# Layer 0's scan sum y stored by pairs of batches, and ScalarE's wait moved to the scatter's own semaphore

## The reference

```python
xn = layernorm(x)
delta = softplus(xn @ W_xproj[:64].T @ W_dt.T + b_dt)        # per token and channel
for t in range(512):                                           # along each batch
    h = exp(delta[t] * A) * h + (delta[t] * xn[t]) * B[t]      # N = 16 states a channel
    y[t] = sum_n h[n] * C[t, n]
x = x + y + xn * D_param + experts(xn)                         # 4 of 16 experts a token
```

## Time and profile before

| | |
|---|---|
| median of 3 runs | 1266.36 us (1265.95 to 1267.10) |
| the profiled execution, its own time | 1271.14 us |
| its span, first to last instruction | 1269.4 us |
| busy: PE, DVE, ACT, POOL | 1032.2, 916.2, 489.1, 466.8 us |
| DMA engines' time taken by the software queue | 33.5% of the span |
| adds into y, scatters and gathers of layer 0 | 32, 80, 80 |

### The profile page before, as it was taken

One profiled execution on the slowest core, in us unless ns is written; L12 is line 12 of the kernel. 1 busy time (PEld: TensorE's weight loads), 2 busy tenths in 40 slices (PEclk: granted clock), 3 DMA queues, 4 the chain that ended last, 5 costly groups with the idle time before them and its releaser, 6 DMA issues.

```text
span 1269.4 us, 18530 instructions
## 1 busy us (share of the span) xinstructions
PE 1032.2 (81%) x6024; PEld 600.7 (47%) x6024; DVE 916.2 (72%) x1506; ACT 489.1 (39%) x1114; POOL 466.8 (37%) x333
## 2 busy tenths in 40 slices
PE   3987997888887878773587778989889988888895
PEld 2354455444444444442434444555545555455453
DVE  4767768899888889897486655766768666755576
ACT  2200235455544445451130144544554444434442
POOL 0000103788888788762270003222313222123310
PEclk9988999898988889995888889989999999899897
DMA  7950443878878787899620134433433333234413
GB/s 228 366 128 0 126 79 105 148 129 148 147 139 159 127 155 134 147 148 213 134 63 1 26 79 97 97 81 81 100 89 81 90 81 79 64 81 106 95 28 133
DMA packets 111188, 143.25 MB, mean 113 GB/s; under 512 B 30023, under 2 KB 97335, under 8 KB 110903
## 3 DMA queue, kind: packets, MB, share of 16 engines
q0 software_dynamic: 34464, 77.92, 33.5%
q1 hardware_dynamic: 76630, 64.14, 18.1%
HBM read 72.80 MB, written 39.46 MB: 88 GB/s over the span
## 4 chain that ended last, share of the span: by engine, by line
PE 33%; DVE 11%; DMA 5%; ACT 4%; issue 3%; POOL 1%; SPq 1%; ACTq 0%; DVEq 0%; POOLq 0%
PE bank L1846 5%; PE bank L1434 4%; PE bank L1427 4%; PE bank L1890 3%; DMA sum<-yo,to_i 3%; DVE cv L2091 2%; PE bank L698 2%; PE bank L1829 2%; PE bank L1912 2%; PE bank L1876 2%; PE bank L1838 2%; PE bank L1870 1%; PE bank L686 1%; DMA x<-sum 1%; DVE areaD L2036 1%
## 5 line engine op out<-in xcount | busy, mean ns | idle before, releaser
L1500 POOL DMA_INDIRECT sum<-yo,to_i x48 | 76.9, 1602 | 361.4 <-ACT yo L1454 359.1
L1164 POOL DMA_INDIRECT sum<-yo,to_i x80 | 156.0, 1950 | 47.5 <-issue 39.9
L1171 POOL DMA_INDIRECT xg<-xn_d,token_i x80 | 103.1, 1289 | 174.7 <-DVE to_i L460 92.2
L1011 PE MATMUL bank<-areaA,xgT 128*128 x320 | 133.0, 545 | 15.2 <-issue 8.8
L1028 PE MATMUL bank<-areaA,hidT 88*128 x320 | 96.7, 427 | 41.5 <-ACT hidT L1076 29.8
L2036 DVE TENSOR_TENSOR areaD<-areaD,gb 128x512 f32<-128x512 f32 x128 | 87.5, 689 | 41.9 <-ACT areaD L1983 32.8
L1144 DVE TENSOR_TENSOR_SCAN xnT<-areaB,xnT 128x1024 f32<-128x1024 f32 x42 | 96.3, 2292 | 3.3
L1028 PEld LDWEIGHTS bank<-areaA,hidT 88*128 88x128 f32 x320 | 57.7, 201 | 76.5 <-issue 71.4
L1983 ACT ACTIVATE areaD<-bank 128x512 f32<-128x512 f32 x128 | 76.1, 594 | 44.7 <-PE bank L1838 42.6
L1011 PEld LDWEIGHTS bank<-areaA,xgT 128*128 128x128 f32 x320 | 62.9, 215 | 61.6 <-issue 46.6
L686 PE MATMUL bank<-xnT,areaB 128*128 128x512 f32 x192 | 86.8, 599 | 0.8 <-DVE y L716 0.8
(11 more groups left out here) (338 smaller groups left out, 2201.9 us busy)
## 6 DMA issues: line engine op xcount, KB each, us to landing
y<-xnT POOLq DMA_DIRECT2D x21, 1024.0 KB
wst<-gu_f SPq DMA_DIRECT2D x96, 176.0 KB
y<-areaB POOLq DMA_DIRECT2D x11, 1024.0 KB
wst<-down_f SPq DMA_DIRECT2D x48, 176.0 KB
areaA<-in_gu SPq DMA_DIRECT2D x2, 2816.0 KB
gu_f<-in_gu POOLq DMA_DIRECT2D x1, 5632.0 KB, 16.8
sum<-yo SPq DMA_DIRECT2D x2, 2176.0 KB, 16.2
down_f<-in_down POOLq DMA_DIRECT2D x1, 2816.0 KB, 22.5
```

Of the source, the lines that this page charges most:

```text
L1011: last = nc.tensor.matmul(bank[:, GB + q % 2, 0:2 * FI], xgT[:, q % 2, k, :], wgu0_of(e, k), start=(k == 0), stop=(k == KD - 1))
L1164: nc.gpsimd.indirect_dma_start(sum0_d[q % 2], bass.IndirectOffsetOnAxis(ap=to_i[:, q:q + 1], axis=0), yo[:, q % 5, :], None, compute_op=AL ...
L1171: nc.gpsimd.indirect_dma_start(xg[:, q % 5, :], None, xn_d[0], bass.IndirectOffsetOnAxis(ap=token_i[:, q:q + 1], axis=0)).then_inc(s.gathe ...
L1500: nc.gpsimd.indirect_dma_start(sum1_d, bass.IndirectOffsetOnAxis(ap=to_i[:, q:q + 1], axis=0), yo[:, q % 4, :], None, compute_op=ALU.add). ...
```

## The change

`y` becomes [128, 2 pairs of batches, 2 halves, 1024 tokens]. A pair's two halves are then adjacent in a partition, and both sides of the add's DMA are one run of 8192 bytes a partition: 128 runs instead of 256, the same bytes. What writes and reads `y` elsewhere (the first fill on ACT, the 32 transposing products of `scan_out_tensor` on PE) follows the new layout. `yo_free` is dropped: ACT waits for the landing of scatter q - 5 itself, on the DMA's semaphore, and POOL no longer counts `yo_free`, in both layers.

```diff
--- before.py
+++ after.py
@@ -159,7 +159,7 @@
             self.tanh_ready, self.hid_ready, self.hT_full = sem(f"tanh_ready{l}"), sem(f"hid_ready{l}"), sem(f"hT_full{l}")
             self.hT_ready, self.y_full, self.y_ready = sem(f"hT_ready{l}"), sem(f"y_full{l}"), sem(f"y_ready{l}")
             self.gathered = [sem(f"gathered{l}_{s}") for s in range(RING[l])]
-            self.combined, self.yo_free = sem(f"combined{l}"), sem(f"yo_free{l}")
+            self.combined = sem(f"combined{l}")
             self.added = [sem(f"added{l}_{k}") for k in range(2 - l)]
             self.sum_out = sem(f"sum_out{l}")
             if l == 1:
@@ -757,8 +757,8 @@
         parts = sb("parts", [3 * 2 * N0, T], BF16, c0)
         delta = sb("delta", [P, 2, T], F32, c0)
         dx = sb("dx", [P, 2, T], F32, c0)
-        y = sb("y", [P, 2, T], F32, c0)
-        shT0 = y[:, :, :].rearrange("p h t -> p (h t)").rearrange("p (f t) -> p f t", t=512)
+        y = sb("y", [P, 2, 2, LB], F32, c0)
+        shT0 = y[:, :, :, :].rearrange("p b h t -> p (b h t)").rearrange("p (f t) -> p f t", t=512)
         drT = dx[0:R0, 1, :]
         odd_sum = areaA[:, 0:TT * D].rearrange("p (t d) -> p t d", d=D)
         after = M0 + m0["words"]
@@ -1079,7 +1079,7 @@
 
             act.wait_ge(s.y_full, q + 1)
             if q > 4:
-                act.wait_ge(s.yo_free, q - 4)
+                act.wait_ge(s.added[(q - 5) % 2], 16 * ((q - 5) // 2 + 1))
             nc.scalar.activation(yo[:, q % 5, :], bank[:, HY, 0:D], ACT.Copy, scale=slot_w[:, q % 5:q % 5 + 1]).then_inc(s.y_ready, 1)
 
         def layer0_scalar(act):
@@ -1089,7 +1089,7 @@
             decay(act, 0)
             act.wait_ge(s.sh_out, NB * 4)
             for hf in range(2):
-                nc.scalar.activation(y[:, hf, :], xnT[:, hf, :], ACT.Copy, scale=d_par[:, hf:hf + 1]).then_inc(y_init, 1)
+                nc.scalar.activation(y[:, :, hf, :], xnT[:, hf, :].rearrange("p (b t) -> p b t", t=LB), ACT.Copy, scale=d_par[:, hf:hf + 1]).then_inc(y_init, 1)
                 if hf == 0:
                     xT_copy(act, 0)
             act.wait_ge(delta_ready, 4)
@@ -1149,18 +1149,17 @@
 
         def add_scan(pool, pair):
 
-            n, hf, at = unit_views(2 * pair)
             pool.wait_ge(hc_ready, 2 * pair + 2)
             if pair > 1:
                 pool.wait_ge(y_added[pair % 2], 16 * (pair // 2))
-            nc.gpsimd.dma_start(y[:, :, at], h_pair[pair % 3], accum_op=ALU.add).then_inc(y_added[pair % 2], 16)
+            nc.gpsimd.dma_start(y[:, pair % 2, :, :].rearrange("p h t -> p (h t)"), h_pair[pair % 3].rearrange("p h t -> p (h t)"),
+                                accum_op=ALU.add).then_inc(y_added[pair % 2], 16)
 
         def scatter_add(pool, q):
 
             pool.wait_ge(s.y_ready, q + 1)
             if q > 1:
                 pool.wait_ge(s.added[q % 2], 16 * (q // 2))
-                pool.sem_inc(s.yo_free, 1)
             nc.gpsimd.indirect_dma_start(sum0_d[q % 2], bass.IndirectOffsetOnAxis(ap=to_i[:, q:q + 1], axis=0),
                                          yo[:, q % 5, :], None, compute_op=ALU.add).then_inc(s.added[q % 2], 16)
 
@@ -1214,7 +1213,7 @@
                     pe.wait_ge(x_back[t // 4], 32)
                 nc.tensor.matmul(bank[:, XB + t % 4, 0:D], ident[:, :], odd_sum[:, t, :], start=True, stop=False)
                 for hf in range(2):
-                    last = nc.tensor.matmul(bank[:, XB + t % 4, hf * P:(hf + 1) * P], y[:, hf, t * P:(t + 1) * P], ident[:, :],
+                    last = nc.tensor.matmul(bank[:, XB + t % 4, hf * P:(hf + 1) * P], y[:, t // 8, hf, t % 8 * P:(t % 8 + 1) * P], ident[:, :],
                                             start=False, stop=(hf == 1))
                 last.then_inc(yT_full, 1)
 
@@ -1450,7 +1449,7 @@
             if part == 2 and 1 <= q <= NT1:
                 act.wait_ge(q1.y_full, q)
                 if q > 4:
-                    act.wait_ge(q1.yo_free, q - 4)
+                    act.wait_ge(q1.added[0], 16 * (q - 4))
                 nc.scalar.activation(yo[:, (q - 1) % 4, :], bank[:, EB + (q - 1) % 2, 0:D], ACT.Copy,
                                      scale=slot_w[:, (q - 1) % 4:(q - 1) % 4 + 1]).then_inc(q1.y_ready, 1)
             if part == 2 and q < NT1:
@@ -1496,7 +1495,6 @@
             pool.wait_ge(q1.y_ready, q + 1)
             if q:
                 pool.wait_ge(q1.added[0], 16 * q)
-                pool.sem_inc(q1.yo_free, 1)
             nc.gpsimd.indirect_dma_start(sum1_d, bass.IndirectOffsetOnAxis(ap=to_i[:, q:q + 1], axis=0),
                                          yo[:, q % 4, :], None, compute_op=ALU.add).then_inc(q1.added[0], 16)
```

## The result

The changed kernel takes 1248.3 us (median of four runs, 1245.6 to 1256.5) against 1266.2 for the kernel before beside it (1264.9 to 1267.1): a ratio of 0.9867, with a 95% interval of 0.9831 to 0.9903. It is 1.3% faster. I had forecast 1265.0 with a range that ended at 1261.8, so the sign was within what I allowed and the size was not.

What follows compares the result with a forecast made beforehand. The prediction took the loop as paced by DVE and its round trip through PE and ACT. Terms 0 + 0 + 0.9 + 0.5 = 1.4 us took 1266.36 to 1265.0 us, range 1261.8 to 1267.8.

Steps and rivals of the forecast that it cites:

- The semaphore, 0: Both layers: ACT's wait for yo_free was never held (17 ns each time), so dropping it gains 0.
- The add on the DMA engines, 5.8 to 5.57 us: Each add of y: 8 KB packets save 0.23 us, taken as 0.25, with bounds of 0 and 0.7.
- rival C: Add's transfer and POOL issue both save near their upper bounds: 3.5 to 4.4 us, 1262.8 to 1262.0; chance 0.31.
- Rival B: Packets get no cheaper, as the queue cuts 8 KB runs or the skill's rule holds: 0.1 us, 1266.2; chance 0.14.
- The rule of the Trainium skill: Small descriptors cost extra only in HBM, not within on-chip memory; by it the add keeps its 5.8 us.
- The forecast's straight line: DMA packet time from 1 and 4 KB: fixed part 0.029 us a packet, so 0.696 us for 8 KB.
- The issue on POOL, 0.2 us less: POOL's issue of each add, 1.28 to 1.9 us, falls by 0.2 with 128 fewer runs; bounds 0 and about 0.65.
- The loop's end, 1.4 us: Adds 27 to 29 and the loads behind them: PE's step 8 comes 0.9 + 0.5 = 1.4 us sooner.
- the engines' start: DMA engines at the loop's end: with SP's loads issued 1.35 us sooner, full data flow starts 0.9 us sooner.
- the stretch of full DMA engines up to PE's step 8: From 582.10 to 604.20 adds 30 and 31 and loads fill the engines; the two adds save 0.5 us.
- In the loop both are hidden by DVE's pace: 0 us for adds 0 to 26: Layer 0's loop: savings in the add's transfer and POOL issue gain nothing there, since DVE sets the pace.
- Both of my conditions for being wrong: DVE's loop end moves over 1 us, showing dependence on POOL or queue; or time after changes by more than 1.4 us.

Runs made afterwards that it cites:

- e2_sem: Kernel before with the semaphore part alone: ACT waits on the scatter's own semaphore, y laid out as before; ratio 1.0007 to the kernel before.
- e7_pool: Changed kernel with five small memsets of an unused tile on POOL ahead of each add; ratio 0.9896 to the kernel before.
- e5: Kernel before with TensorE's and ACT's register loads of the expert number issued early, TensorE loading once per tile; ratio 1.0016 to the kernel before.
- e9: Kernel before with two unread 128x128 matmuls more for each tile, where TensorE waits; ratio 1.0043 to the kernel before.
- e3: Changed kernel with unused words in y, so that adds go in 4 KB runs again; ratio 0.9999 to the kernel before.
- e4: Kernel before with the last product of dx made twice on DVE, so that the loop begins later; ratio 1.0015 to the kernel before.
- e1_layout: Changed kernel with yo_free, its waits and increments kept as before, so the layout alone; ratio 0.9884 to the kernel before.
- e15_pe_dose_new: Changed kernel with TensorE's register load of the expert number ahead of gate_up made twice; ratio 1.0342 to the kernel before.
- e13_pe_early_old: Kernel before with TensorE's register loads alone issued early, ACT's left as they were; ratio 1.0008 to the kernel before.
- e16: Kernel before with all register loads early, the same kernel as e5 run once more under the profiler; 1264.9 us in one run.
- e12_early_busy_new: Changed kernel with the early register loads and two unread matmuls more for each tile; ratio 0.9895 to the kernel before.
- e10: Changed kernel with two unread 128x128 matmuls more for each tile, where TensorE waits; ratio 0.9830 to the kernel before.

## Why the prediction was wrong

**The semaphore, 0:** right. e2_sem gives 1.0007, and ACT's wait stays at 17 ns.

**The add on the DMA engines, 5.8 to 5.57 us:** mis-sized. From its first packet to its last, add 29 takes 5.9 us before and 5.3 after, and over all adds the median falls from 6.3 to 5.8. The rate while it is nearly alone is 197 GB/s against 181 in the earlier trace rows; a packet takes 646 ns in the median against two of 366. The saving is 0.5 to 0.6, at rival C's size. Rival B falls in both its forms. The rule of the Trainium skill (DMA: Bandwidth & Descriptors, Why small descriptors are slow) does not hold between 4 and 8 KB for an add from on-chip memory to on-chip memory. By packets it does not hold at 2 KB either (8, 4 and 2 KB take 646, 366 and 189 ns, which is 646, 732 and 756 for the same 8 KB), but the whole add is as long in 2 KB runs as in 4 KB ones. The forecast's straight line, a fixed part for every packet, is therefore not borne out below 4 KB.

**The issue on POOL, 0.2 us less:** mis-sized, 1.28 to 0.92 at the loop's end. It fits the upper half of the bounds. Whether it matters in the loop e7_pool was too weak to show; e5 and e9 have the fast rhythm at 4 KB, without the shorter issue.

**The loop's end, 1.4 us:** near in number, 1.8 measured, but by luck. With the measured savings, about 0.6 and 0.4 us an add, the forecast's own sum gives some 3.7: 2.5 sooner at the engines' start and 1.2 for two adds. The start did come 2.4 us sooner: the engines are full from 10.0 us ahead of DVE's last product, where it was 7.6. But the stretch of full DMA engines up to PE's step 8, which was to become 0.5 us shorter, is 22.9 us long against 22.1:

```profile
564.10:587.00 22.90, 11.03 (x50) 9.23 (x51) 14.40 (x20) 1.45 (x2) 1.80 (x2) 0.58 1.00 271
```

The two terms were wrong in opposite directions, and 1.7 us are left at step 8.

**"In the loop both are hidden by DVE's pace: 0 us for adds 0 to 26":** this is the step that failed. By the two profiles 16.7 us lie there, and 11 to 15 against e2, e3 and e4. I had shown that nobody waits for an add, a gather or a scatter, and concluded that the adds touch nobody. e1_layout and e3_pad show that the length of a run alone carries the gain. Two things were wrong with the step.

First, the pace was not DVE's work alone. I called the loop "paced by DVE and its round trip" and then left out the round trip; DVE had 43 us in the loop in which it did nothing, and the 27.9 us of the earlier trace rows were the sign. TensorE's part of that round trip is shown to set the pace: e15_pe_dose_new makes the loop 0.77 us longer for each load more, and at 4 KB the fast rhythm comes back both when TensorE's loads are moved (e13_pe_early_old) and when its gaps are filled (e9_busy_old, loads untouched). What the longer runs change there is above all TensorE's time at 1.2 GHz, 59 us in place of 97, and with it DVE's wait for ACT, 12.0 in place of 27.9.

Second, the room that I saw in the queue was room at the slow rhythm. All four executions of 4 KB kernels that ran fast (e5, e16, e9, e13) had gathers land 0.4 us ahead of their use in the end, and none of these kernels is faster than before. So the old kernel had two limits at nearly the same height. The longer run lifts both; the other edits tried on the old layout lift one. With e12_early_busy_new the second shows at 8 KB too.

Both of my conditions for being wrong came true. DVE's end moved by 15.6 us, where 1 was allowed, but only half for the reason in it: nothing in the loop was seen to wait for an add in before, and gathers came late only where the loop ran fast or the runs were 2 KB. The time after DVE's end changed by 5.2 us, of which 3.4 lie in the part that the change does not touch.

**How the 16.7 us divide** is not settled. Two to six of them are before's own distance from e2, e3 and e4. The 38 us less at the lower clock are worth some 8 by e10's rate of 0.2, or 11 by e9's in the first 15 pairs (7.2 us for 25). The loads at line 1008 sum to 44.7 us in before and to 41.9 in the changed kernel, 3 us at most by e15's one for one; in e10 they sum to 49.7, more than in before, and the kernel is the fastest.

**How the length of a run reaches TensorE's clock stays open.** An add does act on instructions that wait for nothing: TensorE's register loads take 0.3 us by themselves, 0.9 inside a 4 KB add and 0.8 inside an 8 KB one. That the long ones set off the falls of the clock was my idea, and the order in time speaks against it (nine of eleven falls come before TensorE stands idle for the load). That these loads hold TensorE back a little and so make falls likelier is possible; no run changed them by so little and nothing else. Other ways were not tried: the adds' moments, which shift when POOL issues them sooner, or POOL's later gathers and scatters. Why an add of 256 packets holds up a register load for longer than one of 128, by 0.1 us in the mean, was not tried either.

## What to carry to other kernels

Before a transfer is written off as hidden because nobody waits for it, look at what the sequencers do while it runs: loads of registers are in no row of busy time, and here they got three times as long under a large transfer. When the engine that sets the pace is idle for a tenth of a loop, the rest of its round trip is part of the pace, the granted clock of the engine in it too. Take "slack" as slack at the present pace: if the change can speed the loop up, ask again whether the queue still fits. When a fix brings nothing, look in its profile for the next limit before dropping it; here early loads brought nothing on the old layout, though they shortened its loop by 16 and 22 us. And when two events stand together, check which of them comes first before one is called the cause.

## What the runs showed of the hardware that I had not expected

- A register load from on-chip memory by TensorE's or ACT's sequencer takes 0.3 us in the mean while no add is on the DMA engines, 0.8 to 0.9 while a 1 MB add runs, and up to 1.5.
- An add from on-chip memory to on-chip memory is not all bytes: packets of 2, 4 and 8 KB take 756, 732 and 646 ns for 8 KB, and the whole 1 MB at its quietest 5.9, 5.9 and 5.2 us.
- TensorE's clock can lock in with a loop: in before it fell to 1.2 GHz for 10.2 us every 37.5 us, five times in a row, and three pairs then took about 3.4 us more (37.4 against 34).
- From kernel to kernel, 15 pairs took 0.36 us more for each microsecond that TensorE spent at 1.2 GHz; where the gaps were filled on purpose, 0.2 to 0.3.
- 160 matmuls of no use in TensorE's gaps made a kernel faster: granted clock 0.97 in place of 0.92, loop 7.4 us shorter.
